# Corner tables for a bilinear gather, laid out in pairs of x corners

## The chip, the cores and the metric

The kernel runs on one core of one Trainium2 chip. The metric is the device time of the whole launch in microseconds (us). Of the kernel before there are three runs, and one more execution that the hardware profiler recorded.

## The reference

Eight images of 512 channels by 32x32 pixels go through four layers, each of them `x = x + layer(groupnorm(x))`:

- layer 0, a state-space block on three resolutions (convolutions, four recurrences over 16 states, norms, a gated projection);
- layer 1, attention with eight heads;
- layer 2, a deformable convolution (DCNv3). Cut to what matters here:

```
xp   = groupnorm(x) @ in_w + in_b              # 32x32 pixels, 16 groups of 32 channels, zero border
t    = gelu(layernorm(depthwise3x3(groupnorm(x))))
off, mask = t @ off_w + off_b, softmax(t @ mask_w + mask_b)   # 9 points for each pixel and group
p    = pixel + grid + off;  p0 = floor(p);  w = p - p0
samp = v00(1-wx)(1-wy) + v01 wx(1-wy) + v10(1-wx)wy + v11 wx wy   # four corners of xp
out  = (sum over the 9 points of mask * samp) @ out_w + out_b
```

- layer 3, a weighted Gram matrix and 20 steps of a power iteration.

All of it is float32. A sample is thus a sum over 9 points x 4 corners = 36 blocks of 32 channels, each block times its own weight.

## The kernel before, in words

**The table.** For each image `l2_prepare_in` (L1266) writes a corner table into device memory: one row of 128 floats for each (y, x, group) of a 33x33 grid, which holds the four corners one after the other, as (corner, channel). The rows of `xp` come from TensorE in eight tiles of 128 pixels (L1325 to L1333, five matmuls each, four PSUM banks in turn). ScalarE copies each to one of four SBUF buffers (L1363), from the fifth on only when the stores of the buffer's last user have landed (L1362). SyncE (L1303 to L1314) then issues 16 DMAs per tile: four image rows times four corners, each moving 32 pixels x 16 groups in runs of 32 floats. Border entries stay zero from `zero_tables`. Beside this, VectorE makes the depthwise convolution in PSUM, first channel tiles 0 and 1, then 2 and 3 (L1393 to L1417); ScalarE copies the sums out (L1366), behind all eight copies of `xp` in its order, and VectorE can start tiles 2 and 3 only when tiles 0 and 1 have left PSUM (L1405). Later VectorE turns offsets and masks into row numbers and weights (L1437 to L1477, `idx` and `wts` in L1493 to L1497).

**The gather.** `Gather` (L90 to L200) does the sampling of an image in 128 units, a unit being 128 pixels of one group. A unit has 9 indirect DMAs, issued by GpSimd (L133), each fetching 128 table rows of 512 bytes into one of `NG` = 5 SBUF buffers `gat`. VectorE then multiplies the 36 blocks by their weights in place (L164, weight broadcast over 32 channels) and sums them to 32 channels (L170). The sum reads `gat` as (channel, block): its innermost run steps by 32 floats:

```
nc.vector.tensor_tensor(v, v, wv, ALU.mult).then_inc(self.prod, 1)
nc.vector.tensor_reduce(bd.dcn[m % 2][:, g * CG:(g + 1) * CG],
                        gat[:].rearrange("p (k c) -> p c k", c=CG), AX.X, ALU.add).then_inc(self.summed, 1)
```

In some stages ScalarE weighs the first 10, 12 or 20 blocks of each unit instead (L150, `blocks=`). GpSimd may start unit n only when unit n-5 is summed (L129), and within a stage its DMAs are also held to "ticks" that ScalarE grants (L132), so that at most four to five units lie between GpSimd and VectorE; below, this distance is called the lead.

**The order of the work.** The gather of image b runs beside the other layers of image b+1 and the end of image b: table L1843 (`BESIDE`) gives each stage its number of units (45 in the recurrence "scan", 30 in attention, 16 in "prepare", 27 in all the rest before the scan, and so on), and `Spread` (L230) places them between the stage's own VectorE instructions. A stage ends in a barrier of TensorE, ScalarE, VectorE and SyncE (`Stage`, L203), GpSimd is outside it. A new gather starts in the stage "finish", after `idx` (L1493). Image 0 is prepared with no gather beside it. Images 1 to 7 each have the gather of the image before beside them. The gather of image 7 runs beside seven power iterations (`layer3_end`), and what is left of image 7 comes last. In the scan VectorE's own work for each of 84 runs is a scan (L864), a product (L841) and, for every tile, another product (L832).

Of the kernel before, what the change touches and what calls it, by code (L numbers as in the profile page):

```python
# [17 lines left out]
P = 128  # L18
# [71 lines left out]
class Gather:  # L90
# [49 lines left out]
    def scale(self, act, done, of):  # L140
# [4 lines left out]
        for n in range(self.scaled_to, goal):  # L145
            gat, (blocks, _) = bd.gat[n % self.NG], self.split[n]
            act.wait_ge(self.gathered[n % self.NG], 16 * KP * (n // self.NG + 1))
            for k in range(blocks):
                block, i = gat[:, k * CG:(k + 1) * CG], n * KP * 4 + k
                ins = nc.scalar.activation(block, block, ACT.Copy, scale=weights[:, i:i + 1])  # L150
# [3 lines left out]
    def weigh(self, dve):  # L154
# [124 lines left out]
class Builder:  # L279
# [85 lines left out]
    def constants(self, ctx):  # L365
# [5 lines left out]
        self.ones = self.sb(ctx, "ones", [P, P])  # L371
        self.sel = self.sb(ctx, "sel", [3 * BC, BC])
# [18 lines left out]
        with nc.Block() as block:  # L391
# [12 lines left out]
            def _(dve):  # L404
# [9 lines left out]
                dve.wait_ge(vorder, 7)  # L414
# [851 lines left out]
    def l2_prepare_in(self, ctx, b):  # L1266
# [5 lines left out]
        xp = [self.sb(ctx, f"xp{i}", [P, C]) for i in range(4)]  # L1272
        x1 = self.sb(ctx, "x1", [P, CT, N])
        sqs = self.sb(ctx, "sq", [P, 2, N])
        sq = [sqs[:, i, :] for i in range(2)]
        sd = self.sb(ctx, "sd", [P, N])
        rs = self.sb(ctx, "rs", [P, N])
# [10 lines left out]
        names = ("xp_done xp_ready dw_sum dw_ready mean2_done cent2 sq2_ready var2_done sd2_ready norm2 gelu_out "  # L1288
                 "om_done om_ready e2_in e2_out l2_order").split()
        (xp_done, xp_ready, dw_sum, dw_ready, mean_done, cent, sq_ready, var_done, sd_ready, normed, gelu_out,  # L1290
         om_done, om_ready, e_in, e_out, order_s) = [self.sem(n) for n in names]
        stored = [self.sem(f"table_stored{i}") for i in range(4)]
        om = self.sb(ctx, "om", [P, PT, NOFF + NMSK])
        pos = self.sb(ctx, "pos", [P, PT * NOFF])
        flo = self.sb(ctx, "flo", [P, PT * NOFF])
        tmp = self.sb(ctx, "tmp", [P, PT * NOFF])
        ints = self.sb(ctx, "ints", [P, PT * NOFF], I32)
        mx = self.sb(ctx, "mx", [P, PT * G])
        table = io["tables"][bass.ds(b % SLOTS, 1)].rearrange("s (y x g) (k c) -> (s y) x g k c", y=TW, x=TW, k=4)
        low = om[:].rearrange("p m f -> p (m f)")[:, PT * NMSK:2 * PT * NMSK]  # L1300
        rowf = om[:].rearrange("p m f -> p (m f)")[:, 0:PT * NMSK]
        with Stage(nc) as block:
            def store(sp):  # L1303
                sp.wait_ge(self.table_zero, 16 * 2)
                for m in range(PT):

                    sp.wait_ge(xp_ready, m + 1)
                    for yy in range(4):
# [7 lines left out]
                for i in range(4):  # L1316
                    sp.wait_ge(stored[i], 16 * 16 * (PT // 4))
# [670 lines left out]
```

## Time and profile before

| | us |
|---|---|
| median of 3 runs | 13847.79 (13846.44 to 13850.41) |
| the profiled execution, as timed | 13856.55 |
| its span in the profile | 13854.9 |
| VectorE busy | 9752.7 (70%) |
| GpSimd busy | 9276.9 (67%) |
| TensorE busy | 8459.1 (61%) |
| ScalarE busy | 4858.1 (35%) |

The span goes from the first to the last instruction. All durations below come from the profiled execution. GpSimd's busy time is nearly all the issue of the 9216 indirect DMAs, and the time between two of them with nothing to wait for is listed as "issue", beside its busy time. The busy shares are averages over stages whose limits differ, so the rows below are taken by stage.

### The profile page before, as it was taken

The numbers are of one execution on the slowest core, as the hardware profiler recorded it, in microseconds if no ns is written. First come the engines' busy times: TensorE is split into PE (matmuls) and PEld (weight loads), VectorE is DVE, ScalarE is ACT, GpSimd is POOL, SyncE is SP. The second block draws the span as 40 slices with busy tenths as digits, with TensorE's granted clock in tenths as the row PEclk, the third lists the DMA queues.
The fourth block names the chain that finished last, engine by engine and source line by source line (L and its number), as shares of the span: only waits on it lengthen the run. The fifth ranks groups of instructions, "written<-read, shape, count | busy, mean of one in ns | idle before, by whom it ended". The sixth has DMA issues, their size and how long they took to land. (4 is left out here: it accounts for less than half of the span.)

```text
span 13854.9 us, 109997 instructions
## 1 busy us (share of the span) xinstructions
PE 8459.1 (61%) x32544; PEld 4121.3 (30%) x32544; DVE 9752.7 (70%) x9864; ACT 4858.1 (35%) x13537; POOL 9276.9 (67%) x9221
## 2 busy tenths in 40 slices
PE   5783657356665558456665568456665567466667
PEld 3241324132332324232332324232232324222223
DVE  6745986569775987669775987669775887644443
ACT  3232543145331543145331553145321553122221
POOL 0005777777777777777777777777777777777771
PEclk7896778667887679767887679767887679788888
DMA  1002121421133111421233111421233111432221
GB/s 72 9 22 66 54 62 53 117 81 53 60 86 110 53 52 60 115 82 53 60 86 110 52 52 59 111 84 54 60 86 110 52 53 60 109 129 81 96 83 49
DMA packets 905628, 1001.99 MB, mean 72 GB/s; under 512 B 697681, under 2 KB 707921, under 8 KB 893074
## 3 DMA queue, kind: packets, MB, share of 16 engines
q0 software_dynamic: 294912, 604.57, 15.3%
q1 hardware_dynamic: 610066, 389.88, 9.2%
q8 instruction: 271, 4.44, 0.1%
q14 instruction: 379, 3.10, 0.1%
HBM read 814.38 MB, written 179.39 MB: 72 GB/s over the span
## 5 line engine op out<-in xcount | busy, mean ns | idle before, releaser
L133 POOL DMA_INDIRECT gat<-corner_tables,idx x9216 | 9276.4, 1007 | 4277.2 <-issue 2772.3
L170 DVE TENSOR_REDUCE dcn<-gat 128x32 f32<-128x1152 f32 x1024 | 2162.2, 2111 | 287.8 <-ACT gat L150 254.3
L150 ACT ACTIVATE gat<-gat,wts 128x32 f32<-128x32 f32 x8752 | 1905.4, 306 | 639.0 <-DMA gat<-corner_tables,idx 638.3
L797 PE MATMUL PS<-hc,ident 128*128 128x512 f32 (+2 forms) x4096 | 1965.3, 640 | 242.4 <-DVE hc L841 199.8
L164 DVE TENSOR_TENSOR gat<-gat,wts 128x1152 f32<-128x1152 f32 (+3 forms) x1024 | 1094.8, 1069 | 942.0 <-DMA gat<-corner_tables,idx 827.8
L864 DVE TENSOR_TENSOR_SCAN hs<-dA,PS 128x1024 f32<-128x1024 f32 x672 | 1531.3, 2279 | 45.5 <-ACT dA L814 18.1
L797 PEld LDWEIGHTS PS<-hc,ident 128*128 128x128 f32 x4096 | 1017.2, 281 | 866.1 <-issue 475.5
L1152 ACT ACTIVATE E<-PS,nmax 128x1024 f32<-128x1024 f32 x512 | 570.5, 1114 | 876.1 <-DVE nmax L1209 737.1
L1073 PE MATMUL PS<-ident,E 128*128 128x128 f32 x4096 | 591.6, 291 | 357.3 <-ACT ET L1142 203.6
L841 DVE TENSOR_TENSOR hc<-hs,PS 128x1024 f32<-128x1024 f32 x672 | 801.6, 1193 | 0.8 <-PE PS L776 0.8
L1742 PE MATMUL PS<-late_M,wp 128*32 128x512 f32 x4480 | 612.8, 696 | 255.9 <-DVE wp L1783 173.2
L1209 DVE TENSOR_REDUCE nmax<-PS 128x1 f32<-128x1024 f32 x512 | 601.7, 1216 | 198.9 <-PE PS L1062 198.7
L776 PE MATMUL PS<-bc1b,pick 96*128 96x512 bf16 x1024 | 389.0, 480 | 566.4 <-DVE hc L841 566.3
L776 PE MATMUL PS<-bc1f,pick 96*128 96x512 bf16 x1024 | 390.8, 483 | 557.1 <-DVE hc L841 557.0
L1073 PEld LDWEIGHTS PS<-ident,E 128*128 128x128 f32 x4096 | 474.8, 148 | 602.4 <-issue 318.3
L1062 PE MATMUL PS<-kk,q 64*128 64x512 f32 x2048 | 587.9, 698 | 12.8 <-DVE kk L1203 12.8
L1218 DVE COPY ET<-PS 128x512 f32<-128x512 f32 x512 | 347.7, 679 | 322.0 <-PE PS L1073 318.9
L814 ACT ACTIVATE dA<-delta1b,A 128x1024 f32<-128x1024 f32 x256 | 293.8, 1148 | 755.5 <-DVE hs L864 755.5
L814 ACT ACTIVATE dA<-delta1f,A 128x1024 f32<-128x1024 f32 x256 | 293.7, 1147 | 731.0 <-DVE hs L864 731.0
L1047 PE MATMUL PS<-XN,wqkv 128*128 128x512 f32 x1024 | 470.9, 603 | 28.6 <-DVE kk L1203 12.1
L1087 PE MATMUL PS<-ET,vT 128*64 128x256 f32 x4096 | 477.8, 387 | 0.0
L1654 PE MATMUL PS<-U 128*128 128x512 f32 x1024 | 461.0, 614 | 0.0
(251 smaller groups left out, 10996.0 us busy)
## 6 DMA issues: line engine op xcount, KB each, us to landing
gat<-corner_tables,idx POOLq DMA_INDIRECT x9216
corner_tables<-xp SPq DMA_DIRECT2D x1024, 64.0 KB, 2.2
D<-in_dist_dram SPq DMA_DIRECT2D x8, 4096.0 KB, 14.4
keep_scratch<-X SPq DMA_DIRECT2D x15, 2048.0 KB, 12.7
weighted<-M SPq DMA_DIRECT2D x56, 512.0 KB, 2.7
late_M<-weighted SPq DMA_DIRECT2D x7, 4096.0 KB, 14.2
wqkv<-in_qkv_w_dram SPq DMA_DIRECT2D x8, 3072.0 KB, 11.7
X<-keep_scratch SPq DMA_DIRECT2D x12, 2048.0 KB, 21.2
```

The lines of the kernel that those rows point to most:

```text
L133: nc.gpsimd.indirect_dma_start(bd.gat[n % self.NG][:, k * 4 * CG:(k + 1) * 4 * CG], None, bd.rows, bass.IndirectOffsetOnAxis(ap=bd.idx[:, ...
L150: ins = nc.scalar.activation(block, block, ACT.Copy, scale=weights[:, i:i + 1])
L164: nc.vector.tensor_tensor(v, v, wv, ALU.mult).then_inc(self.prod, 1)
L170: nc.vector.tensor_reduce(bd.dcn[m % 2][:, g * CG:(g + 1) * CG], gat[:].rearrange("p (k c) -> p c k", c=CG), AX.X, ALU.add).then_inc(self. ...
L776: mm = nc.tensor.matmul(PS[:, bank + i, j * p.hl:(j + 1) * p.hl], self.pick[:, row:row + 1].to_broadcast([3 * BC, P]), p.bc[:, pos], start ...
L797: mm = nc.tensor.matmul(PS[:, p.ybank(d, h), 0:p.hl], self.ident[:], src[:, j, h * p.hl:(h + 1) * p.hl], start=(c == 0 and j == 0), stop=( ...
L841: nc.vector.tensor_tensor(hc[u % 2][:], hs[u % 2][:], Cb, ALU.mult).then_inc(hc_ready, 1)
L864: nc.vector.tensor_tensor_scan(h_, a_, b_, 0.0, ALU.mult, ALU.add).then_inc(scanned, 1)
L1062: mm = nc.tensor.matmul(PS[:, 2 * r + m, :], q[hp % 2][rows, nt * P:(nt + 1) * P], kk[hp % 2][rows, m * NH:(m + 1) * NH], start=True, stop ...
L1073: mm = nc.tensor.transpose(PS[:, 4 + m // 4, (m % 4) * P:(m % 4 + 1) * P], E[i % 4][:, m * P:(m + 1) * P], self.ident[:])
L1209: nc.vector.tensor_reduce(nmax[:, i:i + 1], PS[:, 2 * r:2 * r + 2, :], AX.XY, ALU.max, negate=True).then_inc(max_ready, 1)
L1742: mm = nc.tensor.matmul(PS[32 * j:32 * j + 32, h, :], wp[:, 4 * s + j, :], M[:, 4 * s + j, h * NH:(h + 1) * NH], start=(s == 0), stop=(s = ...
```

## The change

A table row now holds (y corner, channel, x corner): the left and the right corner of a channel stand side by side. For that `xp` is kept in SBUF for all eight tiles as pairs (pixel value, right neighbour's value). The right neighbour is made on TensorE: tile `xp` times a fixed 128x128 matrix `right` (the identity, shifted by one pixel within each image row of 32, last column zero), one float32 matmul a tile, copied back by ScalarE into the second place of each pair. The column left of the image gets an extra tile `edge` (32 rows, from a product of its own). SyncE stores 2 + 8 x 8 = 66 DMAs an image in runs of 64 floats in place of 128 DMAs in runs of 32. VectorE's product views `gat` as (q, channel, pair), and its sum reads (channel, q, pair), so that its innermost run is of two neighbouring floats; ScalarE's blocks are read and written at every second float. ScalarE no longer waits for stores. VectorE waits for all of them before it first writes `tmp`, which now shares memory with `xp`. `pos`, `flo`, `sd` and `rs` move into other buffers. The depthwise sums leave PSUM in the same place of ScalarE's order, behind the `xp` copies, of which there are now 16.

```diff
@@ Gather.scale
-                block, i = gat[:, k * CG:(k + 1) * CG], n * KP * 4 + k
+                block, i = pairs[:, k // 2, :, k % 2], n * KP * 4 + k
@@ Gather.weigh
-        v = gat[:].rearrange("p (k c) -> p k c", c=CG)[:, blocks:, :]
-        wv = bd.wts[:].rearrange("p n (k a) -> p (n k) a", a=1)[:, n * KP * 4 + blocks:(n + 1) * KP * 4, :]\
-            .to_broadcast([P, KP * 4 - blocks, CG])
+        q0 = blocks // 2
+        v = gat[:].rearrange("p (q c a) -> p q c a", c=CG, a=2)[:, q0:]
+        wv = bd.wts[:].rearrange("p n (q o a) -> p (n q) o a", o=1, a=2)[:, n * KP * 2 + q0:(n + 1) * KP * 2]\
+            .to_broadcast([P, KP * 2 - q0, CG, 2])
@@
-                                gat[:].rearrange("p (k c) -> p c k", c=CG), AX.X, ALU.add).then_inc(self.summed, 1)
+                                gat[:].rearrange("p (q c a) -> p c q a", c=CG, a=2), AX.XY, ALU.add)\
+            .then_inc(self.summed, 1)
@@ constants
+                nc.vector.tensor_copy(cols32(self.right)[:, :, 0:W - 1], cols32(self.ident)[:, :, 1:W]).then_inc(vorder, 1)
+                nc.vector.memset(cols32(self.right)[:, :, W - 1:W], 0.0).then_inc(vorder, 1)
@@ l2_prepare_in, SyncE
+                sp.wait_ge(edge_ready, 1)
+                for low in range(2):
+                    sp.dma_start(table[1 - low:H + 1 - low, 0, :, low, :], groups(edge[:])).then_inc(stored, 16)
                 for m in range(PT):
-
                     sp.wait_ge(xp_ready, m + 1)
+                    sp.wait_ge(right_ready, m + 1)
                     for yy in range(4):
-                        y = 4 * m + yy
-                        for corner in range(4):
-                            y0, x0 = y + 1 - corner // 2, 1 - corner % 2
-                            sp.dma_start(table[y0, x0:x0 + W, :, corner, :],
-                                         xp[m % 4][yy * W:(yy + 1) * W, :].rearrange("p (g c) -> p g c", g=G))\
-                                .then_inc(stored[m % 4], 16)
+                        for low in range(2):
+                            sp.dma_start(table[4 * m + yy + 1 - low, 1:TW, :, low, :],
+                                         groups(xp[yy * W:(yy + 1) * W, m, :])).then_inc(stored, 16)
@@ l2_prepare_in, TensorE
+                def shift(m):
+                    pe.wait_ge(xp_ready, m + 1)
+                    if m >= 2:
+                        pe.wait_ge(right_ready, m - 1)
+                    nc.tensor.matmul(PS[:, 2 + m % 2, :], self.right[:], pairs(xp[:, m, :])[:, :, 0],
+                                     start=True, stop=True).then_inc(right_done, 1)
+                nc.tensor.matmul(PS[0:H, 3, :], self.ones[0:1, 0:H], self.inb2[:], start=True, stop=False)
+                for k in range(CT):
+                    mm = nc.tensor.matmul(PS[0:H, 3, :], XN[:, k, 0:N:W], w_in[:, k, :], start=False, stop=(k == CT - 1))
+                mm.then_inc(edge_done, 1)
                 for m in range(PT):
...
                     mm.then_inc(xp_done, 1)
+                    if m == 1:
+                        pe.wait_ge(edge_ready, 1)
+                    if m:
+                        shift(m - 1)
+                shift(PT - 1)
@@ l2_prepare_in, ScalarE
+                act.wait_ge(edge_done, 1)
+                act.wait_ge(edge_zero, 1)
+                nc.scalar.activation(pairs(edge[:])[:, :, 1], PS[0:H, 3, :], ACT.Copy).then_inc(edge_ready, 1)
                 for m in range(PT):
                     act.wait_ge(xp_done, m + 1)
-                    if m >= 4:
-                        act.wait_ge(stored[m % 4], 16 * 16 * (m // 4))
-                    nc.scalar.activation(xp[m % 4][:], PS[:, m % 4, :], ACT.Copy).then_inc(xp_ready, 1)
+                    nc.scalar.activation(pairs(xp[:, m, :])[:, :, 0], PS[:, m % 2, :], ACT.Copy).then_inc(xp_ready, 1)
+                    if m:
+                        shifted(m - 1)
+                shifted(PT - 1)
+                summed(0)
+                summed(2)
@@ l2_prepare_in, VectorE
+                nc.vector.memset(pairs(edge[:])[:, :, 0], 0.0).then_inc(edge_zero, 1)
...
+                dve.wait_ge(stored, 16 * stores)
```

`shifted(m)` is ScalarE's copy of the shift's result into `pairs(xp[:, m, :])[:, :, 1]`, `summed` its copies of the depthwise sums.

## Rows read from the trace of the kernel before

**Rows 1.** The page: busy time, share of the span and instructions of each engine.
```profile
PE 8459.1 (61%) x32544; PEld 4121.3 (30%) x32544; DVE 9752.7 (70%) x9864; ACT 4858.1 (35%) x13537; POOL 9276.9 (67%) x9221
```

**Rows 2.** The page's groups: count, busy us, mean ns, idle before and releaser.
```profile
L133 POOL DMA_INDIRECT gat<-corner_tables,idx x9216 | 9276.4, 1007 | 4277.2 <-issue 2772.3
L170 DVE TENSOR_REDUCE dcn<-gat 128x32 f32<-128x1152 f32 x1024 | 2162.2, 2111 | 287.8 <-ACT gat L150 254.3
```

**Rows 3.** GpSimd's L133 from one start of a gather to the next: length, busy.
```profile
1156.30:2668.50 1512.20, 1151.61 (x1152) 0.75 0.24 66
...
7355.60:8919.00 1563.40, 1165.25 (x1152) 0.77 0.26 74
...
12038.80:13574.40 1535.60, 1137.49 (x1152) 0.82 0.30 98
```

**Rows 4.** Waits of GpSimd over the period 6050 to 7614: us, times, longest.
```profile
POOL gat L133 <- issue: 345.0, 1126, 2.0
POOL gat L133 <- DVE dcn L170: 32.4, 16, 13.0
POOL gat L133 <- DVE idx L1493: 10.7, 1, 10.7
POOL gat L133 <- ACTq L328: 7.8, 9, 5.4
```

**Rows 5.** The same waits, first interval 1156 to 2668.
```profile
POOL gat L133 <- DVE dcn L170: 1.8, 6, 0.3
```

**Rows 6.** The same waits, second interval 2668 to 4229.
```profile
POOL gat L133 <- DVE dcn L170: 28.6, 12, 13.0
```

**Rows 7.** The same waits, last interval 12039 to 13575.
```profile
POOL gat L133 <- DMA gat<-corner_tables,idx: 28.9, 7, 5.4
```

**Rows 8.** Windows (length, busy PE, PEld, DVE, ACT, POOL): scan alone, scan beside, prepare.
```profile
162.60:571.60 409.00, 297.14 (x896) 143.72 (x896) 377.66 (x258) 116.51 (x200) 0.00 (x0) 0.82 0.00 0
...
6152.30:6691.00 538.70, 340.04 (x896) 166.13 (x896) 497.11 (x348) 306.75 (x1100) 398.26 (x417) 0.74 0.18 53
...
7160.20:7354.40 194.20, 81.69 (x176) 34.23 (x176) 138.63 (x104) 26.03 (x27) 135.37 (x120) 0.70 0.44 88
```

**Rows 9.** VectorE's groups of the gather in that scan, by form.
```profile
L170 DVE TENSOR_REDUCE dcn<-gat 128x32 f32<-128x1152 f32 x45 | 94.8, 2107 | 9.8 <-ACT gat L150 8.1
...
L164 DVE TENSOR_TENSOR gat<-gat,wts 128x512 f32<-128x512 f32 x45 | 31.0, 689 | 0.0
```

**Rows 10.** Lines of VectorE by step in SBUF: ns, least, median and most.
```profile
L1472 DVE TENSOR_REDUCE mx<-tmp x8: 1340/1342/1352, 1149.4 to 12024.6; 128x128 f32<-128x1152 f32 x8
...
L1476 DVE TENSOR_TENSOR om<-tmp,pos x8: 1347/1348/1357, 1153.2 to 12034.3; 128x1152 f32<-128x1152 f32 x8
...
L1494 DVE TENSOR_TENSOR wts<-tmp,pos x8: 2205/2206/2216, 1157.0 to 12039.5; 128x1152 f32<-128x1152 f32 x8
```

**Rows 11.** Groups by form: a windowed operand (992 = 32 runs of 31) and a flat one.
```profile
L1409 DVE SCALAR_TENSOR_TENSOR PS<-XN,cols,PS 128x992 f32<-128x992 f32 x128 | 152.4, 1244 | 0.0
...
L1678 DVE SCALAR_TENSOR_TENSOR fd<-PS,sqb 128x1024 f32<-128x1024 f32 x64 | 77.9, 1218 | 135.5 <-PE PS L1654 135.5
```

**Rows 12.** Timeline of prepare, 7160 to 7354, engine by engine: start, us, idle before.
```profile
7172.47 0.60 ACT L1363 ACTIVATE xp<-PS 128x512 f32<-128x512 f32 x1 [4.08 <-PE PS L1331]
...
7219.90 0.60 ACT L1363 ACTIVATE xp<-PS 128x512 f32<-128x512 f32 x1 [11.83 <-DMA corner_tables<-xp]
...
7221.44 2.59 DVE L1406 TENSOR_SCALAR PS<-XN,cols 128x1024 f32<-128x1024 f32 x2 [29.87 <-ACT x L1366]
...
7314.83 1.34 DVE L1442 TENSOR_REDUCE mx<-om 128x128 f32<-128x1152 f32 x1
...
7168.68 98.53 SPq L1312 DMA_DIRECT2D corner_tables<-xp  x128
...
7234.49 0.94 POOL L133 DMA_INDIRECT gat<-corner_tables,idx  x1 [12.99 <-DVE dcn L170]
...
7331.22 3.08 POOL L133 DMA_INDIRECT gat<-corner_tables,idx  x1 [0.30 <-issue]
```

More of the change, by code:

```diff
@@ L371, in constants @@
         self.ones = self.sb(ctx, "ones", [P, P])
+        self.right = self.sb(ctx, "right", [P, P])
         self.sel = self.sb(ctx, "sel", [3 * BC, BC])
@@ L1271, in l2_prepare_in @@
         w_om = self.sb(ctx, "w_om", [P, CT, NOFF + NMSK])
-        xp = [self.sb(ctx, f"xp{i}", [P, C]) for i in range(4)]
+        xp = self.sb(ctx, "xp", [P, PT, 2 * C])
+        edge = self.sb(ctx, "edge", [H, 2 * C])
         x1 = self.sb(ctx, "x1", [P, CT, N])
-        sqs = self.sb(ctx, "sq", [P, 2, N])
+        sqs = self.sb(ctx, "sq", [P, 4, N])
         sq = [sqs[:, i, :] for i in range(2)]
-        sd = self.sb(ctx, "sd", [P, N])
-        rs = self.sb(ctx, "rs", [P, N])
+        sd, rs = sqs[:, 2, :], sqs[:, 3, :]
         XN = self.sb(ctx, "XN2", [P, CT, N])
@@ L1287, in l2_prepare_in @@
         self.group_norm(ctx, "2", XN, sync=load)
-        names = ("xp_done xp_ready dw_sum dw_ready mean2_done cent2 sq2_ready var2_done sd2_ready norm2 gelu_out "
+        names = ("edge_done edge_zero edge_ready xp_done xp_ready right_done right_ready dw_sum dw_ready mean2_done cent2 sq2_ready var2_done sd2_ready norm2 gelu_out "
                  "om_done om_ready e2_in e2_out l2_order").split()
-        (xp_done, xp_ready, dw_sum, dw_ready, mean_done, cent, sq_ready, var_done, sd_ready, normed, gelu_out,
+        (edge_done, edge_zero, edge_ready, xp_done, xp_ready, right_done, right_ready, dw_sum, dw_ready, mean_done, cent, sq_ready, var_done, sd_ready, normed, gelu_out,
          om_done, om_ready, e_in, e_out, order_s) = [self.sem(n) for n in names]
-        stored = [self.sem(f"table_stored{i}") for i in range(4)]
+        stored = self.sem("table_stored")
+        stores = 2 * (1 + PT * 4)
         om = self.sb(ctx, "om", [P, PT, NOFF + NMSK])
-        pos = self.sb(ctx, "pos", [P, PT * NOFF])
-        flo = self.sb(ctx, "flo", [P, PT * NOFF])
-        tmp = self.sb(ctx, "tmp", [P, PT * NOFF])
+        pos = XN[:].rearrange("p t f -> p (t f)")[:, 0:PT * NOFF]
+        flo = sqs[:].rearrange("p t f -> p (t f)")[:, 0:PT * NOFF]
+        tmp = xp[:].rearrange("p m f -> p (m f)")[:, 0:PT * NOFF]
         ints = self.sb(ctx, "ints", [P, PT * NOFF], I32)
         mx = self.sb(ctx, "mx", [P, PT * G])
-        table = io["tables"][bass.ds(b % SLOTS, 1)].rearrange("s (y x g) (k c) -> (s y) x g k c", y=TW, x=TW, k=4)
+        table = io["tables"][bass.ds(b % SLOTS, 1)].rearrange("s (y x g) (k f) -> (s y) x g k f", y=TW, x=TW, k=2)
+        pairs = lambda z: z.rearrange("p (f a) -> p f a", a=2)
         low = om[:].rearrange("p m f -> p (m f)")[:, PT * NMSK:2 * PT * NMSK]
@@ L1347, in _ @@
                 pe.wait_ge(gelu_out, CT)
-                pe.wait_ge(xp_ready, PT)
+                pe.wait_ge(right_ready, PT)
                 for m in range(PT):
```

28 lines of the change are left out of this document (17 added, 11 removed).

## The prediction

> **What bounds the kernel now.** I read the page's shares first, and they mislead. VectorE is busy 70% of the span and GpSimd 67% [rows 1], so VectorE looks like the engine to relieve. The group of the gather's DMAs says otherwise: beside 9276 us busy, GpSimd has 2772 us of "issue" [rows 2], about 0.30 us ahead of each of 9216 DMAs, in which it waits for nothing. A gather DMA thus costs it 1.007 + 0.30 = 1.31 us, and 9216 of them 12.05 ms. The gathers run from 1156 us to 13574 us [rows 3], so GpSimd is occupied for 97% of that time.
>
> Next the intervals from one gather's start to the next [rows 3]. The first takes 1512 us, the six in the middle (12038.8 - 2668.5) / 6 = 1562 us on average, one of them 1563.4, and the last 1536, each with the same 1152 DMAs. What GpSimd waits for over one middle period is in [rows 4]: 32.4 us in 16 waits for VectorE's sum (all five buffers full, VectorE behind), 7.8 us in 9 waits for ScalarE's ticks, and 10.7 us at the end, where the old image's gather is over and the new row numbers aren't there. In the second interval the first figure is 28.6 us [rows 6]; in the first interval it is 1.8 us in 6 waits [rows 5], which is nothing but the usual 0.3 us each, so there GpSimd never stands still. In the last one its extra waits, 28.9 us in 7, are for its own DMAs, where a power iteration begins [rows 7].
>
> So the kernel is a chain with two owners. Inside the scan VectorE owns the time: 409.0 us alone, 538.7 us with 45 units beside it [rows 8], 2.88 us a unit, and those units' instructions take 2.107 + 0.689 = 2.80 us [rows 9]. Almost every nanosecond of a unit is on the path there. Elsewhere GpSimd mostly owns it. What VectorE can give back is at most what GpSimd now stands still.
>
> **Part 1, the sum (L170).** It takes 2.11 us for 1152 elements at a step of 128 bytes [rows 2]. What the same number costs at other steps: contiguous 1.342 us, two floats apart (8 bytes) 1.348 us, four floats apart (16 bytes) 2.206 us [rows 10]. The trace holds no run of two followed by a jump. Its bounds are 1.34 us (as steps of 8 bytes, which also take two floats out of each 16 bytes) and 2.11 us (no gain), and below, under the rivals, a loss. I take 1.34, since the row that is nearest in what it takes from each 16 bytes is the 8-byte one. That is 0.77 us a unit, 1024 x 0.77 = 788 us of VectorE's busy time.
>
> The Trainium skill, SBUF — State Buffer, section "Door 1: The DMA port swizzle", says that SBUF has lines of 16 bytes, that two hits to a line keep full bandwidth, and that each access which crosses to a new line pays. The first half agrees with the 8-byte and 16-byte rows; the page's claim that four float32 can be strided for free does not. Its second half, taken by itself, would halve the penalty and not remove it; that is a rival below.
>
> **Part 2, the product (L164) and ScalarE's blocks (L150).** Data of the product stay contiguous, only the weight is read as (two weights, repeated 32 times). Bounds: no change, or the price per run in the slower rival. I take nothing: no operand skips memory. ScalarE's 32-element blocks now step by 8 bytes; between no change and twice the element time it is covered in the scan, where ScalarE is busy 306.8 of 538.7 us [rows 8]; its only stall of VectorE there is 8.1 us [rows 9]. Uncovered, it would lengthen the ends of the stages in which VectorE waits for it.
>
> **Part 3, the scan.** 45 x 0.77 = 34.6 us come off VectorE: 538.7 becomes about 504 us. GpSimd works at 398.26/417 + 0.30 = 1.255 us a DMA there [rows 8], so in 504 us it issues 402, and the 45 units need 405. The two are then level: the lead no longer fills up in the scan, and the scan ends with some 2 units of lead where it now has 4.
>
> **Part 4, what the later stages do with it.** A lead smaller by 2 units is 18 DMAs, about 24 us of GpSimd work more to be done between the scan and the end of prepare. It fits where GpSimd now pauses behind the scan: 5.4 us for one tick [rows 4], and 13.0 us in prepare, where VectorE stands 29.87 us [rows 12] and all buffers are full. So the scan's 34 us are kept only as far as GpSimd's pauses reach, and that is the sum I use: per middle interval 32.4 - 16 x 0.3 = 27.6 us, or 28.6 - 12 x 0.3 = 25.0 us in the second; I take their mean, 26.3, plus 7.8 - 9 x 0.3 = 5.1 us of ticks, which are due already once GpSimd runs later. 31.4 x 6 = 188 us. I take off 2 us each for pauses that stay (start of the scan): 176 us. VectorE's other 600 us become waits for gathers.
>
> **Part 5, stage ends.** Where a stage's last act is a unit, the end comes 0.77 us sooner: at the seven changes from one gather to the next, and in seven power iterations. 14 x 0.77 = 11 us. The first and last intervals give nothing else, since there VectorE never holds GpSimd up.
>
> **Part 6, prepare.** TensorE gets 13 more products, a shift for each tile and five for the edge. A tile's five products now take 0.60 + 4.08 = 4.68 us [rows 12], 0.94 us each. From the first copy at 7167.8, that makes 8 x 4.68 for the tiles behind the edge, which takes the cold start's place, plus 8 x 0.94, plus about 1.5 us for the last shift and its copy: 7214. Now the last copy begins at 7219.9, held back 11.8 us by the stores [rows 12]. So the depthwise sums leave 5 to 6 us sooner; if reading or writing every second float cost double (8 x 0.94 + 16 x 0.6 = 17 us at most), they would leave 11 us later. With GpSimd busy throughout, either moves nothing but VectorE's wait: cover is GpSimd's own work, and I book zero. If that cover were gone, it would be 6 us of gain or 11 us of loss an image. For image 0 the stores held the copy less, and I book zero as well. The stores: 128 DMAs are issued over 98.5 us [rows 12]. If the bytes set this, 66 DMAs of twice the size take as long and end near 7283; if the runs set it, half. VectorE's new wait stands ahead of its chain of index work, after its reduce at 7314.8 has its inputs [rows 12], at least 25 us behind the later bound. Queued behind SyncE's stores is only the storing of sampled tiles, which waits for the stage's last unit anyway. The extra edge memset, the copy at the start and the moved buffers are under 1 us.
>
> **Sum.** 176 + 11 = 187 us off 13856.6 (the execution as timed, 1.7 us more than its span) is 13670; that execution stands 8.8 us above the median of the three runs, so against the median 13661. I say 13661 us.
>
> **Rivals.**
> Half the penalty: the page's rule that every crossing pays. The crossings halve, so the sum costs 1.34 + 0.385 = 1.73 us. The scan gives 45 x 0.385 = 17 us; the lead still fills at times, and prepare's earlier copy then shortens GpSimd's pause by 5 us: 22 x 6 + 6 = 138 us, 13710. Against it: the 8-byte row crosses twice as often as the contiguous one and costs the same [rows 10]. By that rule, 13710.
>
> Slower, a price for each run of two. The windowed group with 32 runs of 31 takes 1244 ns; the flat one 1218 for 1024, so some 1185 for 992 [rows 11]: 59 ns for 32 runs, 1.8 ns each. A sum has 576 runs of two: 1.34 + 1.06 = 2.40 us; the product of 16 blocks has 256, +0.47 us. Together 0.76 us a unit more in the scan, 34 us a scan, 7 scans: 238 us, 14086. It decides as soon as sum and product together pass the present 2.80 us, which is 1.0 ns a run. Against it: the reduce at L1472 goes in runs of nine and takes 1342 ns, the flat L1476 1348 [rows 10]; 128 runs there cost nothing.
>
> Pauses that stay: the gain of the scan is lost to waits for gathers in it (ScalarE, in order, waits for a block to be gathered and holds back the next `dA`), while prepare keeps its pause. Then only the scan's part of the pauses goes, 32.4 - 13.0 - some 5 = 14 us a period: 6 x 14 + 11 = 95, 13753.
>
> Faster, a cheaper gather: if the halved store traffic is what makes GpSimd's DMAs dear in prepare (135.37/120 = 1.13 us, against 0.955 in the scan [rows 8]), 120 x 0.17 x 6 = 125 us more: 13536. Against it: DMAs of 3.08 us stand at 7331 [rows 12], over 60 us after the stores' end.
>
> **How the numbers follow.** Forecast 0.66, half the penalty 0.12, pauses that stay 0.08, slower 0.08, faster still 0.06. The predicted time is the likeliest's, 13661. The range 13605 to 13755 takes the first three, with 5 us more or less a period for the forecast and some of the cheaper gather; 14 in 100 lie outside. 0.2% is 28 us, about what a measurement of this kernel can tell from no change. Faster 0.88, same 0.04 (a price per run that just eats the gain), slower 0.08.
>
> **What would show it.** L170 at 1.34 us mean; the scan at 502 to 510 us; GpSimd's waits for VectorE's sum in a middle period under 8 us; middle intervals near 1531 us; the first still near 1511; GpSimd's mean per DMA within 0.01 of 1.007; VectorE's waits for gathers up by hundreds of us; its wait in prepare for the depthwise copy 5 us shorter; no wait of VectorE for the table's stores. Wrong if L170 stays over 1.6 us, if the scan falls and prepare or attention grows by more than it gave, or if GpSimd's DMAs change their price.

## The result, and the profile after

The changed kernel takes 13633.74 us (median of 4 runs, 13620.17 to 13645.68) against 13847.12 us, a ratio of 0.9847 with a 95% interval of 0.9835 to 0.986. The forecast was 13661 us in a range of 13605 to 13755. The profiled execution has a span of 13624.3 us.

The page of the kernel after, engines and groups (count | busy us, mean ns | idle before, releaser); L172, L166 and L151 are the sum, the product and ScalarE's blocks:

```profile
PE 8520.4 (63%) x32752; PEld 4123.7 (30%) x32752; DVE 8980.9 (66%) x9874; ACT 4912.7 (36%) x13609; POOL 9244.1 (68%) x9221
...
L133 POOL DMA_INDIRECT gat<-corner_tables,idx x9216 | 9243.7, 1003 | 4079.0 <-issue 2772.2
L151 ACT ACTIVATE gat<-gat,wts 128x32 f32<-128x32 f32 x8752 | 1919.7, 310 | 879.3 <-DMA gat<-corner_tables,idx 878.8
L166 DVE TENSOR_TENSOR gat<-gat,wts 128x1152 f32<-128x1152 f32 (+3 forms) x1024 | 1093.2, 1068 | 1634.2 <-DMA gat<-corner_tables,idx 1526.4
...
L172 DVE TENSOR_REDUCE dcn<-gat 128x32 f32<-128x1152 f32 x1024 | 1385.2, 1353 | 310.2 <-ACT gat L151 277.0
```

The sum went from 2111 to 1353 ns, 777 us less of VectorE's time. The product kept its time. The kernel became only 213 us faster; most of the rest became waiting, since the product's wait for gathers grew from 828 to 1526 us.

GpSimd by interval, from one gather's start to the next (length, busy; the lines answer to [rows 3]):

```profile
1149.60:2652.20 1502.60, 1143.14 (x1152) 0.76 0.23 67
2652.20:4175.60 1523.40, 1157.68 (x1152) 0.78 0.26 76
...
7230.60:8753.80 1523.20, 1157.84 (x1152) 0.78 0.26 76
...
11807.80:13331.00 1523.20, 1139.70 (x1152) 0.81 0.30 99
```

The six middle intervals take (11807.8 - 2652.2) / 6 = 1526 us, where they took 1562. Six times 36 is 215 us of the 231 us between the two spans. The first gather starts 7 us sooner (in half_sum and no_ticks, which have the same work ahead of it as the kernel after, it starts some 5 us later, so most of this can be chance), the first interval is 10 us shorter, the last one is as long as before when both are counted to the last DMA, and what follows it is too.

GpSimd's waits in the middle interval that begins at 7231 (us, times, longest; compare [rows 4]):

```profile
POOL gat L133 <- issue: 345.6, 1134, 0.3
POOL gat L133 <- DVE idx L1535: 9.8, 1, 9.8
POOL gat L133 <- DMA gat<-corner_tables,idx: 3.9, 3, 2.5
POOL gat L133 <- ACTq L331: 3.0, 10, 0.3
POOL gat L133 <- DVE dcn L172: 2.9, 4, 2.0
```

The 32.4 us for the sum are 2.9, and the ticks' longest wait fell from 5.4 to 0.3 us. All waits other than "issue" went from 53.6 (2.7 us of it for gathers) to 19.6 us. GpSimd is hardly held up by VectorE's sum now, 2.9 us in 4 waits; what VectorE still costs it is the wait for new row numbers between two gathers.

By stage, scan, attention and prepare (length, busy PE, PEld, DVE, ACT, POOL; compare [rows 8]):

```profile
7587.50:8085.10 497.60, 328.64 (x897) 158.74 (x897) 461.95 (x348) 308.45 (x1100) 376.12 (x394) 0.75 0.19 54
8192.10:8545.40 353.30, 297.23 (x1600) 166.53 (x1600) 218.50 (x252) 126.57 (x225) 269.79 (x275) 0.93 0.18 52
8559.20:8752.80 193.60, 94.80 (x202) 38.15 (x202) 126.80 (x105) 31.77 (x36) 146.38 (x130) 0.74 0.37 93
```

The scan fell from 538.7 to 497.6 us. Attention grew from 347.4 to 353.3 us, though VectorE has 22 us less to do in it: 275 DMAs are issued there instead of 260, work that the shorter scan left over. Prepare stayed at 194 us with 130 instead of 120 DMAs.

### The profile page after: what moved, and what is told of

Read it like the earlier page. It is cut to its first block and busy times, and to the rows that moved or that the text cites. A ratio compares the mean times of both kernels' runs of the same rounds, so it can differ in the third digit from the quotient of the medians.

```text
span 13624.3 us, 109343 instructions
## 1 busy us (share of the span) xinstructions
PE 8520.4 (63%) x32752; PEld 4123.7 (30%) x32752; DVE 8980.9 (66%) x9874; ACT 4912.7 (36%) x13609; POOL 9244.1 (68%) x9221
## 5 line engine op out<-in xcount | busy, mean ns | idle before, releaser
L133 POOL DMA_INDIRECT gat<-corner_tables,idx x9216 | 9243.7, 1003 | 4079.0 <-issue 2772.2
L151 ACT ACTIVATE gat<-gat,wts 128x32 f32<-128x32 f32 x8752 | 1919.7, 310 | 879.3 <-DMA gat<-corner_tables,idx 878.8
L166 DVE TENSOR_TENSOR gat<-gat,wts 128x1152 f32<-128x1152 f32 (+3 forms) x1024 | 1093.2, 1068 | 1634.2 <-DMA gat<-corner_tables,idx 1526.4
L804 PE MATMUL PS<-hc,ident 128*128 128x512 f32 (+2 forms) x4096 | 1922.5, 628 | 244.5 <-DVE hc L848 198.1
L172 DVE TENSOR_REDUCE dcn<-gat 128x32 f32<-128x1152 f32 x1024 | 1385.2, 1353 | 310.2 <-ACT gat L151 277.0
L804 PEld LDWEIGHTS PS<-hc,ident 128*128 128x128 f32 x4096 | 983.6, 273 | 825.8 <-issue 442.4
L1579 PE MATMUL PS<-ident,dc 128*128 128x128 f32 x256 | 45.6, 362 | 710.8 <-DMA dc<-sampled 710.8
```

Source lines behind the costliest of these rows:

```text
L133: nc.gpsimd.indirect_dma_start(bd.gat[n % self.NG][:, k * 4 * CG:(k + 1) * 4 * CG], None, bd.rows, bass.IndirectOffsetOnAxis(ap=bd.idx[:, ...
L804: mm = nc.tensor.matmul(PS[:, p.ybank(d, h), 0:p.hl], self.ident[:], src[:, j, h * p.hl:(h + 1) * p.hl], start=(c == 0 and j == 0), stop=( ...
```

## The experiments

Unless an edit says otherwise, the gather, the stages and the shares are those of the kernel that a run starts from.

**The sum by itself.** The kernel before, with the sum over the same floats in their order in memory:

```diff
-                                gat[:].rearrange("p (k c) -> p c k", c=CG), AX.X, ALU.add).then_inc(self.summed, 1)
+                                gat[:].rearrange("p (c k) -> p c k", c=CG), AX.X, ALU.add).then_inc(self.summed, 1)
```

> The kernel before with one edit: the sum reads the same 1152 floats in their order in memory (36 neighbours to each output), so it adds up the wrong blocks and takes 1.34 us; table, stores, prepare stage and everything else stay. Theory 1 (the sum's step in SBUF is all of it, and what it gives is what GpSimd stood still): 13640 to 13665 us, GpSimd's waits for the sum in a middle interval fall from 32 us to under 8, prepare keeps its 12 us waits for the stores. Theory 2 (a real part of the gain, 30 us or more, comes from the stores' halving and from ScalarE's no longer waiting for them): 13670 us or more.

Measured: 13641.07 us, ratio 0.985 (0.9833 to 0.9866), the sum at 1353 ns. Old table, old stores, old prepare stage, and the whole gain of the change is there within the intervals. GpSimd's waits for the sum, interval 5717 to 7244:

```profile
POOL gat L133 <- DVE dcn L170: 2.9, 4, 2.0
```

Theory 2 falls, in this form: where the sum is quick, the other parts are worth nothing that can be measured.

**Everything but the sum.** The kernel after, through the same pairs with the x corner outside:

```diff
-                                gat[:].rearrange("p (q c a) -> p c q a", c=CG, a=2), AX.XY, ALU.add)\
+                                gat[:].rearrange("p (q c a) -> p c a q", c=CG, a=2), AX.XY, ALU.add)\
```

> The kernel after with one edit: the sum goes through the same pairs with the x corner outermost, so its innermost run steps by 64 floats and takes one float out of each pair at a time; same result, same table, same stores. Theory 1: the sum back at 2.11 us and the time at 13820 to 13850 us, middle intervals at 1558 to 1563 us. Theory 2: 13800 us or less, since the prepare stage keeps what it gained. Half the penalty for each crossing of a line would have shown at 1.73 us in the kernel after; here it would give 2.11 us as well.

Measured: 13800.58 us, ratio 0.9967 (0.9955 to 0.998), the sum at 2116 ns. That is 46 us under the kernel before, where theory 1 had at most 27; it lies at the edge of what theory 2 gives. Scan and prepare of this kernel, and two groups of waits, GpSimd's in the interval from 5770 and VectorE's in prepare:

```profile
6128.90:6666.10 537.20, 338.80 (x897) 166.44 (x897) 496.77 (x348) 307.92 (x1100) 398.31 (x418) 0.74 0.19 53
7135.10:7322.30 187.20, 96.47 (x202) 38.92 (x202) 138.76 (x105) 31.79 (x36) 136.20 (x120) 0.75 0.37 92
```

```profile
POOL gat L133 <- DVE dcn L172: 22.9, 16, 5.2
```

```profile
DVE PS L1447 <- ACT x L1389: 22.0, 1, 22.0
```

The scan is back at 537 us. Prepare takes 187.2 us instead of 194.2, since VectorE waits 7.9 us less (22.0 for 29.87 us [rows 12]) and GpSimd's pause there, 13.0 us long, is down to 5.2. Six times 7 us is 42 of the 46; the middle intervals as a whole take 1553 us for 1562. So the rest of the change has a worth of its own, and has it only while the sum is slow: both parts draw on the same pauses of GpSimd. Alone they give 206 and 46 us; together 213, not 252.

**Half the sum.**

```diff
-                                gat[:].rearrange("p (q c a) -> p c q a", c=CG, a=2), AX.XY, ALU.add)\
+                                gat[:].rearrange("p (q c a) -> p c q a", c=CG, a=2)[:, :, 0:KP, :], AX.XY, ALU.add)\
```

> The kernel after, with the sum taken over 9 of its 18 pairs of blocks (the other half is left out), so it takes about 0.75 us, 0.6 us less a unit. Theory 1 (GpSimd owns the intervals now): within 15 us of the kernel after, all of it at stage ends (14 x 0.6 = 8 us), middle intervals 1520 to 1527 us, VectorE's waits for gathers up by 500 us or more. Theory 3 (VectorE still owns the scan): 45 x 0.6 = 27 us a scan less, 190 us in all, 13445 us.

Measured: 13552.16 us, ratio 0.9789 (0.9773 to 0.9806), the sum at 753 ns. Theory 3 falls: 600 us less work for VectorE gave 82 us. But 82 is not 15 either. The page's row for GpSimd:

```profile
L133 POOL DMA_INDIRECT gat<-corner_tables,idx x9216 | 9187.8, 997 | 4056.0 <-issue 2770.8
```

GpSimd is busy 56 us less than in the kernel after, for the same DMAs: 1003 became 997 ns each. That and some 4 us of pauses in each of the six middle intervals make up the gain. GpSimd still owns the time, but its price depends on what VectorE does. This led to the cuts below.

**Steps and runs, measured by themselves.** A `probe` called in the constants stage, VectorE instructions one after the other, 1024 floats each, on one buffer `x`:

```diff
+        total(x[:, 0:1024].rearrange("p (c k) -> p c k", c=32))
+        total(x[:, 0:2048:2].rearrange("p (c k) -> p c k", c=32))
+        total(x[:, 0:3072:3].rearrange("p (c k) -> p c k", c=32))
+        total(x[:, 0:4096:4].rearrange("p (c k) -> p c k", c=32))
+        total(x[:, 0:1024].rearrange("p (k c) -> p c k", c=32))
+        total(x[:, 0:1024].rearrange("p (q c a) -> p c q a", c=32, a=2), AX.XY)
+        total(x[:, 0:1024].rearrange("p (q c a) -> p c a q", c=32, a=2), AX.XY)
+        total(x[:, 0:1024].rearrange("p (q c a) -> p c q a", c=32, a=4), AX.XY)
+        total(x[:, 1:1025].rearrange("p (q c a) -> p c q a", c=32, a=2), AX.XY)
+        total(x[:, 0:2048].rearrange("p (n r) -> p n r", r=4)[:, :, 1:3].rearrange("p (c q) a -> p c q a", c=32), AX.XY)
...
+            go(nc.vector.tensor_tensor(z, x[:, 0:4096:4], x[:, 0:1024], ALU.mult))
...
+            go(nc.vector.tensor_tensor(x[:, 0:4096:4], z, z, ALU.mult))
...
+            go(nc.vector.tensor_tensor(x[:, 0:2048:2], z, z, ALU.mult))
```

> The kernel after with 40 VectorE instructions of 1024 floats ahead of it, three of each kind, to measure steps and runs in SBUF by themselves; time some 60 us more than the kernel after. Sums to 32 outputs, innermost step 1, 2, 3, 4 and 32 floats; runs of two at a jump of 64; the same with one float of each pair at a time; runs of four at a jump of 128; runs of two shifted by one float, so that half of them lie across a 16-byte line; runs of two inside every 16 bytes with a gap before and behind. If two floats out of each 16 bytes are enough: 1.21 us for steps 1 and 2 and for every run of two or more that lies in one line, 1.9 us for steps 4 and 32 and for single floats, something between for step 3 and for the runs that lie across. If each crossing is paid: step 2 dearer than step 1 and runs of four dearer than step 1. Then products with a contiguous operand, one read at step 4, one written at step 4 and one written at step 2: 1.2, 1.9, 1.9 and 1.2 us by the rows of the kernel before.

The ten sums in the order of the diff, three of each (ns, least/median/most, first and last start), and then products with a strided input, a strided output, and an output at step 2:

```profile
L453 DVE TENSOR_REDUCE dcn<-X x3: 1220/1220/1221, 12.1 to 14.6; 128x32 f32<-128x1024 f32 x3
L453 DVE TENSOR_REDUCE dcn<-X x3: 1220/1220/1220, 15.8 to 18.3; 128x32 f32<-128x1024 f32 x3
L453 DVE TENSOR_REDUCE dcn<-X x3: 1497/1497/1497, 19.6 to 22.6; 128x32 f32<-128x1024 f32 x3
L453 DVE TENSOR_REDUCE dcn<-X x3: 1944/1944/1945, 24.2 to 28.1; 128x32 f32<-128x1024 f32 x3
L453 DVE TENSOR_REDUCE dcn<-X x3: 1861/1861/1862, 30.1 to 33.9; 128x32 f32<-128x1024 f32 x3
L453 DVE TENSOR_REDUCE dcn<-X x3: 1219/1220/1220, 35.8 to 38.3; 128x32 f32<-128x1024 f32 x3
L453 DVE TENSOR_REDUCE dcn<-X x3: 1865/1867/1867, 39.6 to 43.4; 128x32 f32<-128x1024 f32 x3
L453 DVE TENSOR_REDUCE dcn<-X x3: 1219/1220/1220, 45.3 to 47.8; 128x32 f32<-128x1024 f32 x3
L453 DVE TENSOR_REDUCE dcn<-X x3: 1436/1439/1441, 49.0 to 52.0; 128x32 f32<-128x1024 f32 x3
L453 DVE TENSOR_REDUCE dcn<-X x3: 1220/1221/1221, 53.4 to 56.0; 128x32 f32<-128x1024 f32 x3
...
L469 DVE TENSOR_TENSOR gat<-X x3: 1959/1962/1969, 61.0 to 65.0; 128x1024 f32<-128x1024 f32 x3
L471 DVE TENSOR_TENSOR X<-gat x3: 1973/1973/1976, 67.0 to 71.0; 128x1024 f32<-128x1024 f32 x3
L473 DVE TENSOR_TENSOR X<-gat x3: 1225/1226/1227, 73.0 to 75.5; 128x1024 f32<-128x1024 f32 x3
```

Runs of two cost what contiguous floats cost, 1.22 us, at both jumps tried (64 floats, and 4 from the middle of one 16 bytes to the next), and a float by itself costs 1.86 to 1.94 us. What fits these rows: two neighbours in the order of reading that share 16 bytes (a line) go at full rate. Step 2 and the pair in the middle of 16 bytes are full; step 3, where every second pair of reads shares a line (1.50), and the runs shifted by one float (1.44), half of which lie across, stand between. Both lie nearer the full rate than half way to the row of single floats (1.54 us), so the reading gives the order of the rows and not every size. Writing follows the same rule: step 4 costs 1.97, step 2 costs 1.23. Paying for each crossing is out, since step 2 crosses twice as often as step 1 at the same time. The Trainium skill's line of 16 bytes with at least two hits in it (SBUF — State Buffer, "Door 1: The DMA port swizzle") agrees with all of this; its free step of four floats (1.94 us here) and its price for each crossing don't.

**A ninth of GpSimd's work taken away**, on both kernels:

```diff
-        rows = [(n, k) for n in range(self.issued, min(self.units, self.target + self.NG - 1)) for k in range(KP)]
+        rows = [(n, k) for n in range(self.issued, min(self.units, self.target + self.NG - 1)) for k in range(KP - 1)]
```

(the waits count 16 x 8 and not 16 x 9, and the buffers start as zeros)

> The kernel before without the ninth DMA of each unit (the ninth point's samples stay zero): GpSimd has 1024 DMAs less to issue, 1.31 us each. Theory 1: where VectorE owned the time (the scan and the 44 us of pauses, 27 us of them for the sum) nothing is gained, elsewhere something is. GpSimd needs 144 x 1.31 = 189 us less an interval; VectorE's own work sets in long before that is used up, first of all in the scan, which stays at 535 to 540 us. I expect 13000 to 13500 us, and GpSimd's waits for the sum up to 60 us or more an interval. If GpSimd were no limit: 13830 us or more.

> The same on the kernel after. Theory 1 (after the change GpSimd is the only owner of the middle intervals): this gains more than it did on the kernel before, as the sum's 0.77 us in the scan are now usable: the scan at 500 to 506 us, and the distance between the two kernels grows from 213 us to 280 us or more. Theory 3 (VectorE still owns the scan of the kernel after): both gain the same, and the distance stays at 213 us.

Measured: 13534.46 us (ratio 0.9776, 0.9759 to 0.9792) and 12984.79 us (0.9378, 0.9363 to 0.9394). The first is 34 us over the range that was expected. The same relief gives 312 us before the change and 649 us after it, and the distance between the two kernels is 550 us where it was 213. Between the profiled spans, the six middle intervals give 116 us before the change and 379 after it. The scans, first before, then after, and GpSimd's waits for the sum in one middle interval each:

```profile
6042.10:6580.10 538.00, 338.33 (x896) 165.70 (x896) 496.83 (x348) 306.74 (x1100) 351.70 (x367) 0.75 0.16 47
```

```profile
POOL gat L133 <- DVE dcn L170: 177.9, 52, 27.6
```

```profile
5803.40:6304.60 501.20, 326.90 (x897) 159.20 (x897) 462.56 (x348) 307.48 (x1100) 349.86 (x369) 0.76 0.18 50
```

```profile
POOL gat L133 <- DVE dcn L172: 103.3, 32, 21.0
```

Before the change, the scan doesn't care about 11% fewer DMAs: 538 us, VectorE's. After it, it stands at 501 us, VectorE's own again. That is the two-owner reading with its sign: VectorE's limit for the scan lies at 500 us, and the kernel after sits right on it, with GpSimd at the same pace.

**The shift made dear.**

```diff
-                    nc.tensor.matmul(PS[:, 2 + m % 2, :], self.right[:], pairs(xp[:, m, :])[:, :, 0],
-                                     start=True, stop=True).then_inc(right_done, 1)
+                    for again in range(3):
+                        mm = nc.tensor.matmul(PS[:, 2 + m % 2, :], self.right[:], pairs(xp[:, m, :])[:, :, 0],
+                                              start=True, stop=True)
+                    mm.then_inc(right_done, 1)
```

> The kernel after with each shift product made three times over (the same result): 16 more float32 products an image on TensorE, 0.94 us each, 15 us more ahead of the copy that lets VectorE go on in prepare. Theory 1 (this lies under GpSimd's work, booked at zero): within 15 us of the kernel after, VectorE's wait in prepare 15 us longer; only image 0, with no gather beside it, pays 15 us. If prepare's TensorE chain is on the path: 8 x 15 = 120 us more.

Measured: 13684.39 us, ratio 0.9883 (0.9867 to 0.99), 50 us more than the kernel after; 35 between the two profiled spans. The profiled execution is the fastest of the four by 20 us, so 15 of the 50 us stand in no trace. Of the 35, image 0 pays 16 (its gather starts at 1166 us, not 1150, of which some 5 can be chance), the first interval 4, and the six middle ones 3 each (1529 for 1526 us); the last one gives 4 back. The expectation had 15 in all. GpSimd's work covers most of every 15 us, not all: with that much delay VectorE falls behind again and GpSimd waits for the sum 8.9 us in the interval where it was 2.9. Its DMAs were also cheaper in this execution, 3.5 us a middle interval, so the delay really showed by 6 to 7 us.

**Ticks taken away** in the power iterations (`ticks=ITERS` to `ticks=0` for that stage).

> The kernel after with the gather beside the seven power iterations no longer held to ScalarE's ticks (ticks=0 for that stage; GpSimd is still held to five buffers). GpSimd's 31 us of pauses in the last interval stand where a power iteration begins, and it waits there for a grant. Theory 1 (GpSimd owns this interval too): most of them go, 20 to 30 us off the kernel after, about 13607 us. If the power iteration's own chain sets its 192 us: no change, and VectorE's waits for gathers shrink instead.

Measured: 13646.05 us, ratio 0.9855 (0.9839 to 0.9872), no gain. GpSimd's waits in the last interval, 11823 to 13346:

```profile
POOL gat L133 <- DMA gat<-corner_tables,idx: 26.8, 7, 5.0
```

The expectation had the wrong cause. The waits stay without grants (27.8 us in the kernel after); GpSimd waits there for its own gathers to land. Each power stage but the last begins with the fetch of a coming image's 6 MB (4096 KB of `late_M` and 2048 KB of `X` or `late_X`), and in the trace of the kernel after six of GpSimd's seven long pauses begin 10 to 12 us behind the issue of a `late_M`. That these transfers hold up the gathers fits the place, but wasn't tried.

**Long instructions cut up.** In the kernel after, 3 of GpSimd's DMAs beside the index work of prepare look like this:

```profile
8724.29 2.99 POOL L133 DMA_INDIRECT gat<-corner_tables,idx  x1 [0.30 <-issue]
8727.58 2.98 POOL L133 DMA_INDIRECT gat<-corner_tables,idx  x1 [0.30 <-issue]
8730.87 3.08 POOL L133 DMA_INDIRECT gat<-corner_tables,idx  x1 [0.31 <-issue]
```

and beside them, on VectorE:

```profile
8723.90 2.56 DVE L1497 TENSOR_TENSOR om<-sq,XN 128x2304 f32<-128x2304 f32 x1
8726.49 2.56 DVE L1498 TENSOR_TENSOR sq<-sq,om 128x2304 f32<-128x2304 f32 x1
...
8730.48 2.56 DVE L1500 TENSOR_TENSOR XN<-XN,sq 128x2304 f32<-128x2304 f32 x1
```

The usual DMA takes 0.944 us. cut_chain cuts such instructions, cut_both the gather's product too:

```diff
+    def cut(self, op, *tiles, pieces=4, keep=True):
+        n = tiles[0].shape[1] // pieces
+        for i in range(pieces):
+            self.mark(op(*[z[:, i * n:(i + 1) * n] for z in tiles]))
+        if keep:
+            self.wait()
...
-                o.step(nc.vector.tensor_tensor(flo[:], flo[:], rnd, ALU.subtract))
+                o.cut(lambda a, b: nc.vector.tensor_tensor(a, a, b, ALU.subtract), flo, rnd)
...
-        nc.vector.tensor_tensor(v, v, wv, ALU.mult).then_inc(self.prod, 1)
+        parts = 1 if blocks == 20 else 3 if not blocks else 2
+        size = KP * 2 - q0
+        for i in range(parts):
+            sl = slice(size * i // parts, size * (i + 1) // parts)
+            ins = nc.vector.tensor_tensor(v[:, sl], v[:, sl], wv[:, sl], ALU.mult)
+        ins.then_inc(self.prod, 1)
```

> The kernel after, with the long VectorE instructions of the index work at the end of prepare and of the weights in finish (14 of them, 1152 or 2304 floats, up to 2.56 us, all on operands in SBUF) each cut into four, the same result. In the trace of the kernel after each GpSimd DMA that overlaps one of them takes 1.2 to 3.1 us in place of 0.944. Theory A (GpSimd's DMA waits until the VectorE instruction with two operands in SBUF, or in its doubled rate, has ended): the long DMAs shrink to 1.0 to 1.5 us, GpSimd's mean in prepare falls from 1.129 to about 1.05 and in finish from 1.39, 8 to 14 us an interval, and as GpSimd owns the intervals the kernel gains 40 to 80 us against the kernel after. Theory B (they are long for another reason, such as the DMAs of the stage or the address stream): mean in prepare stays at 1.12 or more, and the time is that of the kernel after or some 5 us an interval worse for the instructions' own fixed time.

> cut_chain, and also the gather's product in three pieces where VectorE weighs all 36 blocks and in two where it weighs 24 or 26 (in the scan it stays whole, 0.69 us). Theory A: the 1.35 us products delay GpSimd's DMAs too (548 long DMAs overlap one in the kernel after), so another 20 to 50 us go. Theory B, or VectorE's fixed time for 160 more instructions an interval, 0.06 us each on a path: no gain or 10 us an interval lost against cut_chain.

Measured: 13607.00 us (ratio 0.9829, 0.9815 to 0.9842) and 13492.98 us (0.9746, 0.9732 to 0.9759), the latter 141 us under the kernel after. For the kernel after and then for cut_both, GpSimd's windows in prepare, and cut_both's row on the page:

```profile
8559.20:8752.80 193.60, 146.38 (x130) 0.74 0.37 93
```

```profile
6967.80:7158.80 191.00, 132.80 (x130) 0.75 0.38 94
...
L141 POOL DMA_INDIRECT gat<-corner_tables,idx x9216 | 9025.8, 979 | 4159.9 <-issue 2772.6
```

The same 130 DMAs cost 13.6 us less. Theory A holds: a GpSimd DMA waits for the end of such a VectorE instruction beside it, and shorter instructions make shorter waits. For instructions with two operands in SBUF the gather's product shows it, the only thing that differs between cut_chain and cut_both; the index work also holds copies and scalar operations, which weren't cut apart from the rest. The trace of the kernel after says the same: 598 DMAs of more than 1.0 us begin within a gather's product, and they end 0.82 us behind its end (0.81 to 0.82 for nine in ten), however much of it was left. The first DMA shown above does so too: 8724.29 + 2.99 is 0.82 us behind 8723.90 + 2.56. The sizes were off both ways. cut_chain gave 27 us against 40 to 80: GpSimd was 88 us less busy, but its wait for new row numbers between two gathers grew from 9.8 to 20.0 us in a middle interval. These come at the end of VectorE's index work, which the pieces' fixed time makes longer (in cut_both VectorE's work in prepare grew by 5 us); cutting the product gave 114 against 20 to 50. GpSimd's busy time fell by 218 us in all, and nearly two thirds of that reached the kernel's time.

**The cuts on the kernel before, and finer cuts on the kernel after** (six and three pieces for three and two).

> The cuts of cut_both made on the kernel before: same table, sum at 2.11 us. GpSimd's work falls by some 30 us an interval, as it did there, but VectorE owns the scan (538 us) and the first part of what follows. Theory 1 (two owners): well under the 141 us that the cuts gave on the kernel after (13493 against 13634) in the middle intervals, GpSimd's waits for the sum grow from 32 to 45 us or more an interval, 13750 to 13800 us; the change is then worth 260 to 310 us on top of the cuts instead of 213. If GpSimd's price counts in full wherever it stands: 13706 us.

> cut_both with the gather's product in six pieces instead of three, and three instead of two (in the scan still whole). If a GpSimd DMA waits for the running piece alone, the wait halves again, GpSimd's mean falls from 0.979 to about 0.965: 1.0014 x 9216... some 12 to 16 us an interval at most, 80 to 110 us in all, less what VectorE's fixed time of some 230 more instructions an interval (0.06 to 0.1 us each) costs in attention and norms, where it may take over: 13420 to 13500 us. If it comes out over 13510 us, VectorE's fixed time has taken over.

Measured: 13775.81 us (ratio 0.995, 0.9937 to 0.9964) and 13470.57 us (0.9732, 0.9719 to 0.9745). Both kernels have a mean of 979 ns a DMA with the first cuts, but the kernel before gains 68 us by them and the kernel after 141. GpSimd's waits of cut_before in the interval from 5757:

```profile
POOL gat L141 <- DVE dcn L183: 41.6, 15, 22.6
```

What GpSimd saves there is partly waited away: for the sum it waits 41.6 us where it was 32.4, a little less than the 45 expected. On top of the cuts the change is worth 283 us. The finer cuts gave 22 us more, within the expected range, though a DMA's mean fell only to 976 ns and not to 965. cut_both and cut_fine are faster than both kernels of this case.

## Why the prediction was right

**What bounds the kernel**: shown, by a change on each side. Another 600 us less of VectorE's work give 82 (half_sum), 56 of them in the price of GpSimd's DMAs and the rest in its last pauses. Less of GpSimd's work gives twice as much after the change as before it (eight_before, eight_after). VectorE's limit for the scan came out at 538 us before and 501 us after.

**Part 1, the sum**: 1.353 us for a forecast of 1.34, and the bound of 2.11 and both prices of the rivals are out. slow_sum shows what the bound would have given. The nearest row, at steps of 8 bytes, was the right one to trust, and the probe bears it out.

**Part 2**: the product's mean stayed (1069 to 1068 ns). ScalarE's blocks went from 306 to 310 ns, nowhere near double.

**Part 3, the scan**: 504 us forecast, 497.6 and on average 499 measured, a little under the 502 to 510 us that were named as a sign. 394 DMAs were issued in it, for 402.

**Part 4, the pauses**: this term carried the sum, and its mechanism was right. It put the recoverable pauses at 31.4 us a middle interval and took 2 us off for pauses that stay. The six intervals became 35.8 us shorter on average; GpSimd's busy time gave 4.4 of that and the pauses 31.4, the whole of what was found. So 176 us were 188, and 26 us came on top from cheaper DMAs, for which nothing was booked. In the middle interval shown it was 34.0 us of pauses (53.6 to 19.6) and 7.4 us of busy time (1165.25 to 1157.84). "GpSimd's mean per DMA within 0.01 of 1.007" held with 1.003, but 4 ns on 9216 DMAs are 33 us, as much as the forecast was off; a tolerance that looks narrow on one DMA was wide in the sum. Of these 33 us, 21 are no effect of the change that the runs can show. A DMA that nothing holds up took 0.947 us in the median in the trace before and 0.944 in the one after, but it also took 0.947 in no_ticks, with the short sum, and 0.944 in slow_sum, with the long one.

**Part 5, stage ends**: 11 us booked, and no run shows them. The last interval, seven power iterations, took 1523 us in both. The first interval was forecast near 1511 us and took 1502.6; 8.5 of its 10 us are cheaper DMAs (1151.6 to 1143.1 us), not an end. In the spans, 12 us more of pauses, 35 of cheaper DMAs and 7 ahead of the first gather stand against the 11 that didn't come: 231 us for 187. That the forecast came within 27 us of the median is thus in part luck.

**Part 6, prepare**: VectorE waits 24.6 us for 29.87, 5 us less, as worked out. As its three units ahead of the wait are shorter too, it goes on 53.9 us into the stage where it was 61.2, 7 us sooner. The timeline of the kernel after (ScalarE's last copy and the sums behind it, VectorE's restart, SyncE's stores, VectorE's first instruction behind its new wait):

```profile
8611.58 0.62 ACT L1395 ACTIVATE xp<-PS 128x512 f32<-128x512 f32 x1 [0.36 <-PE PS L1339]
8612.09 1.93 ACT L1389 ACTIVATE x<-PS 128x1024 f32<-128x1024 f32 x2
...
8613.14 2.59 DVE L1447 TENSOR_SCALAR PS<-XN,cols 128x1024 f32<-128x1024 f32 x2 [24.60 <-ACT x L1389]
...
8577.96 52.23 SPq L1323 DMA_DIRECT2D corner_tables<-xp  x64
...
8714.48 1.34 DVE L1484 TENSOR_REDUCE mx<-om 128x128 f32<-128x1152 f32 x1
```

The stores' issue takes half the time for the same bytes, so the bytes don't set it. The number of runs and the number of DMAs were both halved, and no run tells which of them does. It ends near 8630, 84 us ahead of the wait. Booking zero for all of this was right in the end and not by itself: slow_sum shows that it is worth 46 us as long as the cover isn't there, the case that the text priced at 6 us an image; shift_three shows that the cover is not complete.

Of the rivals, a price for each run and half the penalty are refuted by the probe, pauses that stay by the waits of the kernel after. The cheaper gather happened in a small way, and not by the mechanism named: prepare's DMAs cost 1.13 us as before. The chances have a slip: the four readings with a faster kernel add up to 0.92, where the last line has 0.88.

## What to carry to other kernels

Add up an engine's time between its instructions before calling it idle: GpSimd was "67% busy" and had 3% to spare. When two engines take turns as owner, a saving on one is worth at most what the other stands still, and two edits that draw on the same pauses don't add up. To make a strided float32 read by VectorE cheap it was enough here that two neighbours in the order of reading lie in the same 16 bytes.

## What was unexpected

- VectorE's instructions set the price of GpSimd's gather DMAs. A 2.56 us instruction with two SBUF operands makes the DMA beside it take 3.0 us in place of 0.944.
- A still shorter sum makes the DMAs cheaper (1.003 and 0.997 us for sums of 1.35 and 0.75 us), but the sum itself doesn't hold GpSimd up: in the trace of the kernel after, the 1030 DMAs that begin within a sum take 0.944 us in the median and 0.96 at most. The saving lies beside the product. What DMAs that begin within a product take above 0.944 us adds up to 307 us in the kernel after and to 233 us in half_sum, where fewer of the long ones begin there (527 for 598) and nearer to its end (0.56 us of it left for 0.64). Why they fall so stays open.
- Together with one point in nine less to fetch the change is worth 550 us: its gain depends on what GpSimd has to do as much as on the instruction that it speeds up.
